# Attention kernel: the product with v moved to three tiles behind its transposes, with a fourth tile buffer and probability buffers of two lengths

## What is computed

```python
def _L0_attn_ref(hidden_states, Wq, Wkr, Wdk, Wupk, Wupv, Wo):
    ...
    scores = jnp.einsum('bhqd,bhkd->bhqk', q, k) * scale
    causal = jnp.tril(jnp.ones((q_len, q_len), bool))
    scores = jnp.where(causal[None, None], scores, jnp.asarray(-1000000000.0, dt))
    attn = jax.nn.softmax(scores, axis=-1)
    out = jnp.einsum('bhqk,bhkd->bhqd', attn, v)
    out = out.transpose(0, 2, 1, 3).reshape(bsz, q_len, N_HEADS * HEAD_DIM)
    return out @ Wo.T
```

## Time and profile before

| | |
|---|---|
| time, median of 3 runs | 2486.45 us (2485.74 to 2490.48) |
| the profiled execution | 2481.92 us, of which the span 2479.7 us |
| TensorE busy, matmul / weight load | 96% / 79% of the span |
| VectorE, ScalarE, GpSimd busy | 60%, 46%, 38% |
| granted TensorE clock, mean | 0.992 |
| chain that ended last | PE 63%, issue 8%, ACT, DVE and DMA 3% each, POOL 1% |

### The profile page before, as it was taken

One profiled execution on the slowest core, in us unless ns is written; L12 is line 12 of the kernel. 1 busy time (PEld: TensorE's weight loads), 2 busy tenths in 40 slices (PEclk: granted clock), 3 DMA queues, 4 the chain that ended last, 5 costly groups with the idle time before them and its releaser, 6 DMA issues.

```text
span 2479.7 us, 38961 instructions
## 1 busy us (share of the span) xinstructions
PE 2370.3 (96%) x11840; PEld 1961.9 (79%) x11840; DVE 1482.2 (60%) x3641; ACT 1134.6 (46%) x2217; POOL 938.5 (38%) x813
## 2 busy tenths in 40 slices
PE   6999999997899999999999999999999999999998
PEld 5777877776688878878887888788888878888876
DVE  4343434423576666666666767676666666676765
ACT  2443625334354544444444545454445444454544
POOL 1000000000454544545454545454444545454543
PEclk9999999999999999999999999999999999999999
DMA  5676767588313121221212042312122121203010
GB/s 192 196 293 168 267 177 254 185 283 330 119 34 112 43 95 52 94 98 41 103 43 104 35 174 86 125 51 94 55 92 88 50 103 43 103 35 111 35 51 18
DMA packets 103736, 287.26 MB, mean 116 GB/s; under 512 B 9056, under 2 KB 42336, under 8 KB 92512
## 3 DMA queue, kind: packets, MB, share of 16 engines
q1 hardware_dynamic: 101408, 280.53, 33.1%
q10 hardware_dynamic: 2112, 4.19, 0.4%
HBM read 200.80 MB, written 83.89 MB: 115 GB/s over the span
## 4 chain that ended last, share of the span: by engine, by line
PE 63%; issue 8%; ACT 3%; DMA 3%; DVE 3%; POOL 1%; DVEq 0%; ACTq 0%; POOLq 0%; SPq 0%
PE ob L1132 14%; PE qb L1079 14%; PE scores L1096 13%; PE ob L1117 12%; PE ptb L1106 8%; DMA ff_raw<-in_ffw 3%; PE ring L848 2%; ACT pT L992 2%; DVE pT L1036 2%; ACT prob L979 1%; POOL prob L953 1%; ACT ff_w L665 0%; DVE nmax L1017 0%; PE ptb L1079 0%; DMA wq<-w_parts 0%
## 5 line engine op out<-in xcount | busy, mean ns | idle before, releaser
L953 POOL TENSOR_TENSOR prob<-prob,rinv 128x896 f32<-128x896 f32 (+7 forms) x512 | 582.7, 1148 | 378.8 <-DVE rinv L1054 374.7
L992 ACT ACTIVATE pT<-ptb 128x512 fp32r<-128x512 f32 x576 | 334.6, 592 | 527.6 <-PE ptb L1106 522.8
L979 ACT ACTIVATE prob<-prob,nmax 128x896 f32<-128x896 f32 (+7 forms) x512 | 396.8, 775 | 362.3 <-DVE nmax L1017 355.2
L1117 PE MATMUL ob<-pT,v_sb 128*128 128x512 f32 x1728 | 507.4, 412 | 17.8 <-DVE pT L1036 15.3
L1036 DVE TENSOR_TENSOR pT<-ptb,pT 128x512 fp32r<-128x512 f32 x576 | 390.4, 687 | 94.8 <-ACT pT L992 86.2
L1017 DVE CUSTOM_DVE_ANT_0 prob<-scores,mask 128x896 f32<-128x896 f32 (+7 forms) x512 | 384.3, 753 | 62.0 <-issue 46.8
L959 POOL TENSOR_TENSOR q_cos<-q_cos,q_sin 128x512 f32<-128x512 f32 x125 | 161.6, 1292 | 591.7 <-DVE q_cos L1032 591.7
L1079 PE MATMUL qb<-xT,wq 128*128 128x512 f32 x1500 | 363.4, 391 | 2.2 <-DVE q_cos L1032 1.3
L1117 PEld LDWEIGHTS ob<-pT,v_sb 128*128 128x128 f32 x1728 | 293.6, 189 | 89.7 <-DVE pT L1036 46.8
L1106 PE MATMUL ptb<-ident,prob 128*128 128x128 f32 x2304 | 340.4, 274 | 6.8 <-POOL prob L953 5.2
L1096 PE MATMUL scores<-kT,late_qT 128*128 128x512 f32 (+3 forms) x1536 | 342.4, 360 | 0.0
(11 more groups left out here) (86 smaller groups left out, 2250.4 us busy)
## 6 DMA issues: line engine op xcount, KB each, us to landing
wq<-w_parts SPq DMA_DIRECT2D x128, 512.0 KB, 3.7
w_parts<-stage SPq DMA_DIRECT2D x32, 1024.0 KB, 4.9
ff_raw<-in_ffw SPq DMA_DIRECT2D x56, 384.0 KB, 4.0
k_parts<-stage SPq DMA_DIRECT2D x128, 128.0 KB, 2.3
v_parts<-stage SPq DMA_DIRECT2D x64, 256.0 KB, 3.6
w_raw<-in_wqo SPq DMA_DIRECT2D x32, 512.0 KB, 5.7
kT<-k_parts SPq DMA_DIRECT2D x16, 1024.0 KB, 7.4
v_sb<-v_parts SPq DMA_DIRECT2D x16, 1024.0 KB, 8.8
```

Of the source, the lines that this page charges most:

```text
L953: nc.gpsimd.tensor_tensor(prob[:, n % 2, h, 0:W], prob[:, n % 2, h, 0:W], rinv[:, hd % 8:hd % 8 + 1].broadcast_to([P, W]), ALU.mult)\
L979: nc.scalar.activation(prob[:, n % 2, j, 0:W], prob[:, n % 2, j, 0:W], ACT.Exp, bias=nmax[:, hd % 8:hd % 8 + 1], scale=-1.0, accum_out=rsu ...
L992: nc.scalar.activation(pT[:, t % 3, HI], ptb[t % 2][:], ACT.Copy).then_inc(pT_hi, 1)
L1117: mm = nc.tensor.matmul(ob[:], v_sb[:, e % 2, x, j], pT[:, t % 3, y], start=(j == 0 and (x, y) == (HI, HI)), stop=(is_last(kind, n, j) and ...
```

## The change

`LAG` goes from 2 to 3, so that three transposes of tiles stand ahead of the first product in place of two. `pT` gets a fourth tile of 4 KB, and the two equal halves of `prob` (16 KB each) become a short buffer of 12 KB for even units and a long one of 16 KB for odd ones. So that even units never have over six key blocks, `ORDER` swaps two query blocks: units now have 4, 3, 2, 1, 5, 7, 6 and 8 key blocks. In the first piece ScalarE also waits for two stores of the stage before ahead of its first tile. The number of matmuls and of other operations is the same. (Left out: five more lines in which `prob[:, n % 2, ...]` becomes `prob[n % 2][:, ...]`.)

```diff
+SHORT = 6 * P
...
-ORDER = (3, 2, 1, 0, 4, 5, 6, 7)
+ORDER = (3, 2, 1, 0, 4, 6, 5, 7)
...
-LAG = 2
+LAG = 3
...
-        pT = sb("pT", 3 * KB, [P, 3, 2, 512], F32R)
-        oT = sb("oT", 15 * KB, [P, 2, 512], F32R)
-        prob = sb("prob", 19 * KB, [P, 2, GRP, S])
+        pT = sb("pT", 3 * KB, [P, 4, 2, 512], F32R)
+        oT = sb("oT", 19 * KB, [P, 2, 512], F32R)
+        prob = [sb("short_prob", 23 * KB, [P, GRP, SHORT]), sb("long_prob", 35 * KB, [P, GRP, S])]
...
                             act.wait_ge(w_kept_lo, SPLIT_BLOCKS * (CHUNKS + 1))
+                            for p in range(2):
+                                act.wait_ge(w_kept[p], 8 * SPLIT_BLOCKS * (CHUNKS + 1))
                         act.wait_ge(t_done, it1 * KEYB + t + 1)
-                        nc.scalar.activation(pT[:, t % 3, HI], ptb[t % 2][:], ACT.Copy).then_inc(pT_hi, 1)
+                        nc.scalar.activation(pT[:, t % 4, HI], ptb[t % 2][:], ACT.Copy).then_inc(pT_hi, 1)
...
-                        nc.vector.tensor_tensor(pT[:, t % 3, LO], ptb[t % 2][:], pT[:, t % 3, HI].bitcast(F32),
+                        nc.vector.tensor_tensor(pT[:, t % 4, LO], ptb[t % 2][:], pT[:, t % 4, HI].bitcast(F32),
...
-                            mm = nc.tensor.matmul(ob[:], v_sb[:, e % 2, x, j], pT[:, t % 3, y],
+                            mm = nc.tensor.matmul(ob[:], v_sb[:, e % 2, x, j], pT[:, t % 4, y],
```

More of the change, by code:

```diff
@@ L494, in turning @@
             if opening and 0 < n < AHEAD:
-                return prob[:, 1, n, 0:512], prob[:, 1, n, 512:1024]
+                return prob[1][:, n, 0:512], prob[1][:, n, 512:1024]
             return q_cos[:], q_sin[:]
@@ L952, in work @@
                         pool.wait_ge(inv_ready, it1 * HPB + hd + 1)
-                        nc.gpsimd.tensor_tensor(prob[:, n % 2, h, 0:W], prob[:, n % 2, h, 0:W],
+                        nc.gpsimd.tensor_tensor(prob[n % 2][:, h, 0:W], prob[n % 2][:, h, 0:W],
                                                 rinv[:, hd % 8:hd % 8 + 1].broadcast_to([P, W]), ALU.mult)\
@@ L978, in work @@
                         act.wait_ge(inv_ready, it1 * HPB + hd - 7)
-                        nc.scalar.activation(prob[:, n % 2, j, 0:W], prob[:, n % 2, j, 0:W], ACT.Exp,
+                        nc.scalar.activation(prob[n % 2][:, j, 0:W], prob[n % 2][:, j, 0:W], ACT.Exp,
                                              bias=nmax[:, hd % 8:hd % 8 + 1], scale=-1.0,
@@ L1016, in work @@
                         nc.vector.memset(seen[:, hd % 8:hd % 8 + 1], 0.0)
-                        nc.vector.tensor_tensor_reduce(prob[:, n % 2, j, 0:W], scores[hd % 2][:, 0:W],
+                        nc.vector.tensor_tensor_reduce(prob[n % 2][:, j, 0:W], scores[hd % 2][:, 0:W],
                                                        mask[:, S - W:], -1.0, 3e38, ALU.add, ALU.min,
@@ L1106, in work @@
                             mm = nc.tensor.transpose(ptb[t % 2][:, h * P:(h + 1) * P],
-                                                     prob[:, n % 2, h, j * P:(j + 1) * P], ident[:])
+                                                     prob[n % 2][:, h, j * P:(j + 1) * P], ident[:])
                         mm.then_inc(t_done, 1)
```

## The result

The changed kernel takes 2469.73 us (median of 4 runs, 2466.27 to 2470.14) against 2487.84 us (median of 4, 2485.74 to 2490.48) for the kernel before in the same comparison: ratio 0.9924, 95% interval 0.9906 to 0.9941. That is 18.1 us, between 15 and 23, where 14.8 was forecast. The profiled execution takes 2466.27 us, 15.7 us less than the 2481.92 us of before.

A forecast was written before the change was run, and what follows sets the result against it. TensorE's matmuls were taken to bound the kernel, so only its stalls could move. The terms -21.8 - 1.1 + 8.0 + 0.1 = -14.8 us gave 2472 us from the median, range 2467 to 2478 us.

The forecast's parts named there:

- What bounds the kernel: TensorE's matmuls fill 96% of the span, so an edit that leaves their number alone can only move stalls.
- no clock change is in play: In the bodies the clock was taken as granted in full, 0.99 to 1.00.
- Part 1: Ends of units of 6, 7 and 8: a third product behind the last transposes, with one more wait gone, gains 22.9 us.
- I take all of it: The stalls at the ends of units of 6, 7 and 8 go entirely: 1.36 us, 16 times, 21.8 us.
- the term of the unit of 8: Unit of 8: the end stall of 0.63 us and the wait of 0.07 us before transposes 6 go.
- Part 2: Head of the unit of 4: transposes 3, directly behind transposes 2, wait for a split; 0.53 us in 15 units, 8.0 us lost.
- Half of a product's restart for four short transposes: Unit of 4: restarting transposes 3 after their wait costs half of the 0.12 us that a product's restart costs.
- The reading that the split stays where it is: Unit of 4: the split of tile 1 comes no earlier, so transposes 3 start 0.47 us late.
- Part 3, the close places: Transposes 4 of the unit of 8 (0.36 us left), NORM (0.7 us left) and other places: no time gained or lost.
- The full gain: Rival: the split of tile 1 comes earlier and the loss at the unit of 4 is nothing; 2463.5 us, chance 0.12.
- No change: Rival: released time meets waits for ptb at transposes 4 of the unit of 8 and like places; 2486 us, chance 0.15.
- Slower, by the starts of bodies: Rival: each start of a body as bad as the worst, 26.6 us more in 7 bodies; 2498 us, chance 0.05.

The follow-up runs named there:

- its two cures: Changed kernel with LAG 2 in units of up to four key blocks, 2464.02 us; changed kernel with W beside units of four moved behind transposes 1, 2461.81 us.

## Why the prediction was right, by its own steps

**What bounds the kernel.** That only stalls of TensorE could move held in the steady steps: counts are unchanged, the clock is granted in full there, and the whole difference is in distances between starts. In the profiled executions it adds up. The steady steps give 2 x 1.01 us less in each of seven bodies, 14.1 us (the sum of eight steps is 113.07 us before and 112.06 after). Six starts of bodies cost 25.6 us over a steady step before and 24.5 after, 1.1 less, with 1.5 in one unit behind a start counted. Together 15.2, as the windows say: 1609.4 - 1594.2 = 15.2. But "no clock change is in play" was not right. The bodies hold three stretches at half clock before and two after, all at starts or just behind one. What one costs shows in the Q behind the fourth start, beside the same 12 matmuls in another body, 4.24 us for 2.72:

```profile
1579.79:1584.03 4.24, 4.24 (x13) 3.36 (x12) 0.85 (x2) 0.84 (x3) 0.61 (x1) 0.62 0.03 6
1461.94:1464.66 2.72, 2.72 (x13) 2.25 (x12) 0.85 (x2) 0.80 (x3) 0.61 (x1) 1.00 0.03 6
```

So the 1.1 us less at the starts are of the size of one such stretch less, which is no part of the forecast's mechanism.

**Part 1.** Forecast 1.36 + 0.07 us a half body, measured 1.52 in the same three units and 0.02 in the unit of five. "I take all of it" was right, since the last product of the unit of 8 had 0.57 us to spare. Slightly mis-sized was the term of the unit of 8, 0.76 us for 0.70, and the units of 6 and 7 together, 0.76 for 0.73; where in them the last 0.1 us stood wasn't followed.

**Part 2.** Forecast 0.53 us, measured 0.48 in the step and 0.45 + 0.06 in the starts. Half of a product's restart for four short transposes was right: the piece from transposes 3 to the product is 0.41 us against 0.35 without a wait. The reading that the split stays where it is because VectorE's maximum waits for scores held: it begins 0.14 us after transposes 2 (1678.38 and 1678.24), before 0.16. The rule of the Trainium skill that was weighed there, Perfetto Trace Analysis, section Optimization Strategy (a gap that repeats on the engine that should be saturated can mean that SBUF or PSUM for the next tile is short), is half right here. The fourth SBUF tile was needed for the distance, by the run with three tiles, which costs 60 us; but four tiles with `LAG` 2 left all 69 gaps in place. And the gap of 0.5 us at the unit of four, which repeats as regularly, went away by a new place for W, with the same two PSUM tiles. A third `ptb` was not run.

**Part 3, the close places.** Forecast 0.36 us left at transposes 4 of the unit of 8, measured 0.32, in order of time on DVE, PEld and PE:

```profile
1662.00 1.28 DVE L1039 TENSOR_TENSOR pT<-ptb,pT 128x512 fp32r<-128x512 f32 x2
```

```profile
1662.78 0.59 PEld L1109 LDWEIGHTS ptb<-ident,long_prob 128*128 128x128 f32 x4
```

```profile
1663.01 0.60 PE L1109 MATMUL ptb<-ident,long_prob 128*128 128x128 f32 x4
```

The first of the two subtractions, that of tile 2, ends at 1662.00 + 0.69 = 1662.69, and transposes 4 start at 1663.01, with no bracket. Forecast 0.7 left at NORM, measured 0.93:

```profile
1653.59 1.89 POOL L954 TENSOR_TENSOR long_prob<-long_prob,rinv 128x1024 f32<-128x1024 f32 x1 [1.54 <-DVE rinv L1057]
...
1656.41 0.82 PE L1109 MATMUL ptb<-ident,long_prob 128*128 128x128 f32 x6
```

It ends at 1655.48 and the transposes start at 1656.41. Both places were passed without a wait, the first by little.

**The rivals.** *The full gain* fell: the `ptb` row of 6.9 us is in the trace, and its two cures bring 2464.02 and 2461.81 us, about the 2463.5 us that this rival gave. *No change* fell, since transposes 4 don't wait; the kernel with three tiles shows what it would have looked like, with the waits for `ptb` as the first row. *Slower, by the starts of bodies* didn't occur: the pieces at "issue" went from 13.4 to 10.7 us. Over the kernels of this study, which differ in a few instructions, they lie between 10.6 and 15.4 us in six pieces (five in one), a spread of 4.8 us. With what stands behind them, the six starts sum to between 24.4 us (three `pT` tiles) and 29.7 us (short units with `LAG` 2) over steady steps, and that spread of 5 us is what the starts can do to a comparison here; the 26.6 us of the rival were never near.

**The size.** -18.1 by medians, -15.7 in the profiled executions, -14.8 forecast. The seven bodies gave 15.2 us where 7 x 1.8 = 12.6 were forecast: 7 x 2 x 0.11 = 1.5 more in the steady steps (1.01 for 0.90) and 1.1 in the starts. Ahead of them and behind them 0.5 us was gained where the rest of the forecast, 2.2, should have come; the stretch ahead of the bodies, with eight stretches at half clock for seven before, took 658.5 us against 657.1, which wasn't followed further. So the mechanism was right, and that the profiled gain came within 0.9 us of the forecast is in part luck: 1.1 us more than forecast from the starts stands against 1.7 less outside the bodies. The 2.4 us between the two measures of the gain are less than the 4.7 us by which executions of the kernel before differ.

## What to carry to other kernels

Count the work on the bound engine between the instruction that makes a tile and the one that needs it, and compare it with the way round over the other engines (here 1.95 us unqueued, plus 0.3 us for the weight load): a distance of three tiles pays only where that way is longer than two, and it needs a buffer more, or the wait moves into the order of the engine that fills the buffers and holds up all behind it. A deeper distance pulls producers together, and each pair of producers that shares a tile then needs other work between; look for a piece to move there before adding a buffer. A stall of 0.3 to 0.6 us looks small and costs up to 10 us when it repeats in 16 half bodies; it shows in starts and in the waits of the weight loads, not in busy shares.

## What the runs showed of the hardware

- A late operand costs more than its lateness on TensorE. Behind a wait, three matmuls of 512 columns took 0.79 to 0.80 us to the next instruction's start where 0.68 is their work (1680.59 to 1681.38 above), and four transposes 0.41 where they take 0.35 to 0.36. In those rows PEld starts together with PE, while elsewhere weight loads run ahead of it.
- The weight load is what has to be on time. It starts 0.23 us ahead of its transposes (1662.78 and 1663.01); the split ended 0.29 us ahead of them in the earlier trace rows and 0.32 us here, and both were free, so all but 0.06 to 0.09 us of those distances was used up.
- Starts of bodies cost 3.3 to 6.7 us each over a steady step in the nine traces. The worst of the six is the same one in all of them, the fourth, where the second batch begins (5.3 to 6.7 us, the others 3.3 to 5.2), and there "issue" ahead of the first scores is a small part (at most 1.2 us). The trace of the changed kernel shows what TensorE waited for: a transfer, a maximum and a split, and VectorE itself at "issue" ahead of another split:

```profile
PEld ob L1135 <- DMA wo_b<-w_parts: 1.2, 1, 1.2
PEld scores L1099 <- DVE nmax L1020: 1.9, 1, 1.9
```

```profile
1572.66 0.69 DVE L1039 TENSOR_TENSOR pT<-ptb,pT 128x512 fp32r<-128x512 f32 x1 [4.09 <-issue]
```

- The idle time at a start can be followed by a lower clock. Behind some starts the granted clock is 0.50 for 3.4 us (the rows are in the section on the result and under what bounds the kernel). In the kernel before, starts with such a stretch cost 4.3 to 4.6 us and those without, the fourth apart, 3.4 to 3.5; which starts get one changes from kernel to kernel (one to four in the seven bodies). The unit of two key blocks behind the fourth start of the changed kernel took 11.21 us where the fifteen others took 9.69 to 9.73, and its Q above has the whole difference.
